# Turned keys of a batch in one row of columns: a change to the two local attention layers of a fused kernel

## The chip, the cores and the metric

The kernel runs as one launch on one core of one Trainium2 chip. The metric is the device time of that launch in microseconds; the kernel before took 1494.41 us (median of three runs, 1487.76 to 1495.81). Names used below: PE is TensorE (PEld its weight loads), DVE is VectorE, ACT is ScalarE, POOL is GpSimd, SP is SyncE, whose queue issues the DMAs. SBUF is the on-chip memory, PSUM the one that matmuls write.

## The reference, cut to what matters

The program is a latent attention with residual, then two "window" layers (local attention and a gated MLP), then a last residual. The change touches only the local attention of the window layers. There are 4 batches of 1024 tokens, width 128, 8 heads of 64, windows of 64 tokens:

```python
def local_attention(q, k, v):                 # WINDOW = 64
    bq = q.reshape(b, h, w, WINDOW, d) * QK_SCALE
    bk = k.reshape(b, h, w, WINDOW, d)
    bv = v.reshape(b, h, w, WINDOW, d)
    def look_around(t):                       # each window sees the one to its left and itself
        p = jnp.pad(t, ((0,0),(0,0),(1,0),(0,0),(0,0)))
        return jnp.concatenate([p[:, :, :w], p[:, :, 1:]], axis=3)
    bk, bv = (look_around(bk), look_around(bv))
    sim = jnp.einsum('bhwid,bhwjd->bhwij', bq, bk)
    mask = (i < j) | (i > j + WINDOW) | (j == -1)
    sim = jnp.where(mask, -jnp.finfo(sim.dtype).max, sim)
    attn = jax.nn.softmax(sim, axis=-1)
    out = jnp.einsum('bhwij,bhwjd->bhwid', attn, bv)
```

Before it q and k are normalised to unit length and rotated (cosine and sine tables); after it come an output projection, a residual, and the MLP.

## The kernel before, in words

`window` (one call per layer, two layers) works on 32 tiles of 128 tokens (two windows each, 8 tiles a batch). Every engine has its own instruction stream, and in each the order is written out by hand in a function `slot(s, ...)`: slot s holds work of several tiles at once (tile s is projected, tile s-2 has its scores, tile s-3 its values, tile s-4 its output). Semaphores alone tie the streams together, and each engine executes its own stream in order.

For a tile the steps are these. PE projects q and k (L892) and v (L896). ACT copies q and k to `raw` (L1006). DVE multiplies `raw` by the cosines (L1133, `cosines`); POOL multiplies it by the sines in four instructions (L1080) and adds the two (L1085, `rotate`). ACT squares and DVE sums (L1124, L1128); POOL raises the sums to the power -1/2 (L1090, `norms`); DVE multiplies the rotated q and k by that (L1142, `normalise`). PE turns q and k so that the 64 numbers of a head lie on partitions (L904, `turn_qk`); ACT copies the turned q (L1022), DVE the turned k (L1148, in `copy_kT`). PE writes the mask (L914) and adds the scores (L921 and L925, `scores`). DVE takes the maxima (L1158), ACT the exponentials (L1029), DVE the reciprocal of the sums (L1168) and the product with it (L1171, both in `divide`). PE turns the probabilities (L936), ACT and DVE copy them (L1036, L1163), and PE multiplies them by v (L951) and by the output weights (L958). DVE adds the result to x (L1175, `residual`).

On DVE a slot runs: `copy_kT(s-2)`, `divide(s-3)`, `residual(s-4)`, `cosines(s)`, first `maxima(s-2)`, `carry(s+2)`, `copy_pT(s-3)`, `normalise(s-1)`, second `maxima(s-2)`, `sums(s)`. On POOL it runs `norms(s-1)` (one L1090), then `rotate(s)` (four L1080, one L1085). `norms` waits for the sums of DVE, `normalise` for `norms`.

The turned keys lie in `kT[P, 2, 4, KEYS]` with KEYS = 192: two buffers that alternate by tile. Columns 0 to 127 are the tile's own two windows; columns 128 to 191 are the second window of the tile before. The second instruction of `copy_kT` (L1151) fetches these 64 columns (of all 4 head pairs, so 256 numbers a partition) out of the other buffer, after a wait for the scores of the tile before, and signals `prev_copied`, for which `scores` waits on PE. The first window of a tile so has its keys in two pieces (own window, then left window) and L921 reads them with a hole in between; the second window's keys are columns 0 to 127. The columns of probabilities, the mask (built on the host) and the values follow that order: `vb` holds for every tile the values of the first window's two pieces, its own on partitions 0 to 63 and the left ones on partitions 64 to 127. Two DMAs a tile (L871, L872, in `spread_v`, on SP's queue) fill it from `v`.

Of the kernel before, what the change touches and what calls it, by code (L numbers as in the profile page):

```python
# [24 lines left out]
B, S, D = 4, 1024, 128  # L25
P = 128
NT = B * S // P
TB = S // P
# [14 lines left out]
DEPTH, HEADS, DH, WIN = 2, 8, 64, 64  # L43
INNER = HEADS * DH
QK_SCALE = 8.0
KEYS = 3 * WIN
# [591 lines left out]
def at_least(eng, sem, base, t, k):  # L638

    if isinstance(t, int) and t + k <= 0:  # L640
        return
    eng.wait_ge(sem, base + t + k)
# [16 lines left out]
def load_mlp_weights(nc, sp, io, sb, layer):  # L659

    w_in, w2, b1 = sb["f_in"], sb["w2"], sb["b1"]
    sp.dma_start(sb["w1"], io["w1"][layer]).then_inc(w_in, 16)
    w2_l = io["w2"][layer]
    sp.dma_start(w2[:, 0:2, :], w2_l[0:2 * HC, :].rearrange("(c p) n -> p c n", p=HC)).then_inc(w_in, 16)
    sp.dma_start(w2[0:HCS[2], 2, :], w2_l[2 * HC:HID, :]).then_inc(w_in, 16)
    b1_l = io["b1"][layer].rearrange("(w n) -> w n", w=2)
    with nc.allow_non_contiguous_dma("a bias to a partition each"):
        for w in range(2):
            for c in range(3):
                sp.dma_start(b1[0:HCS[c], w, c:c + 1], b1_l[w, c * HC:c * HC + HCS[c]].unsqueeze(1)).then_inc(w_in, 16)  # L670
        sp.dma_start(sb["lg"], io["ln_g"][layer].unsqueeze(1)).then_inc(w_in, 16)
        sp.dma_start(sb["lb"], io["ln_b"][layer].unsqueeze(1)).then_inc(w_in, 16)
    sp.dma_start(sb["b2"], io["b2"][bass.ds(layer, 1), :].broadcast_to((P, D))).then_inc(w_in, 16)
    sp.dma_start(sb["shift"], io["c_shift"]).then_inc(w_in, 16)
    sp.dma_start(sb["carry_m"], io["c_carry_m"]).then_inc(w_in, 16)
# [130 lines left out]
def window(nc, io, sb, layer):  # L806
# [5 lines left out]
    base = layer * NT  # L812
    with ExitStack() as ctx:
        def tile(name, shape, dt=F32):
            return ctx.enter_context(nc.sbuf_tensor(f"{name}{layer}", shape, dt))

        def sem(name):
            return sb["kept"]("w_" + name)
# [6 lines left out]
        raw = tile("w_raw", [P, 2, 2 * INNER])  # L825
        t1, t2 = tile("w_t1", [P, 2 * INNER]), tile("w_t2", [P, 2 * INNER])
        rot = tile("w_rot", [P, 2, 2 * INNER])
        qT, kT = tile("w_qT", [P, 2, 4, P]), tile("w_kT", [P, 2, 4, KEYS])
        v = [tile(f"w_v{r}_", [P, INNER]) for r in range(4)]
        vb = [tile(f"w_vb{r}_", [P, INNER]) for r in range(4)]  # L830
        bias = tile("w_bias", [P, 2, HEADS])
# [6 lines left out]
        psT = ctx.enter_context(nc.psum_tensor(f"w_psT_{layer}", [P, 2, 512], F32))  # L838
        psS = ctx.enter_context(nc.psum_tensor(f"w_psS_{layer}", [P, 2, 512], F32))
        psO = ctx.enter_context(nc.psum_tensor(f"w_psO_{layer}", [P, 512], F32))  # L840

        w_in, tables, zeroed = sb["w_in"], sem("tables"), sem("zeroed")
        vb_in = [sem(f"vb_in{r}") for r in range(4)]
        xT_done, hT_copied, carried = sem("xT_done"), sem("hT_copied"), sem("carried")
        qk_done, v_done, sq_done, ss_done, ssm_done, rn_done = (sem(x) for x in ("qk_done", "v_done", "sq_done", "ss_done", "ssm_done", "rn_done"))
        v_copied, raw_done, t1_done, t2_done, rot_done, unit_done = (sem(x) for x in ("v_copied", "raw_done", "t1_done", "t2_done", "rot_done", "unit_done"))
        qkT_done, qT_copied, kT_copied, prev_copied = sem("qkT_done"), sem("qT_copied"), sem("kT_copied"), sem("prev_copied")
        s_done, bias_done, exp_done = sem("s_done"), sem("bias_done"), sem("exp_done")
        rden_done, prob_done = sem("rden_done"), sem("prob_done")
        pT_done, pT_copied = [sem("pT_done0"), sem("pT_done1")], [sem("pT_copied0"), sem("pT_copied1")]  # L850
# [3 lines left out]
        def halves(eng, s, t, k):  # L854

            if isinstance(t, int) and 2 * t + k <= 0:
                return
            eng.wait_ge(s, base * 2 + t * 2 + k)
# [6 lines left out]
        @block.sync  # L865
        def _(sp):
            def spread_v(t, r):

                at_least(sp, v_copied, base, t, 1)
                halves(sp, av_done, t, -4)  # L870
                sp.dma_start(vb[r][0:WIN, :], v[r][0:WIN, :]).then_inc(vb_in[r], 16)  # L871
                sp.dma_start(vb[(r + 1) % 4][WIN:P, :], v[r][WIN:P, :]).then_inc(vb_in[r], 16)  # L872

            sp.wait_ge(zeroed, layer * 4 + 4)
            for t in range(NT):
                if t == 8:
                    load_mlp_weights(nc, sp, io, sb, layer)
                spread_v(t, t % 4)

        @block.tensor  # L880
        def _(pe):
# [25 lines left out]
            def scores(t, r):  # L907
                p = r % 2
                at_least(pe, qT_copied, base, t, 1)
                at_least(pe, kT_copied, base, t, 1)  # L910
                at_least(pe, prev_copied, base, t, 1)
                halves(pe, exp_done, t, 0)
                for w in range(2):
                    pe.matmul(psS[:, w, :].rearrange("p (c k) -> p c k", c=4), sb["ident_b"],  # L914
                              sb["mask_w"][:, t % TB, :].unsqueeze(1).broadcast_to((P, 4, P)), start=True, stop=False, skip_group_check=True)
                for c in range(4):
                    cols = slice(c * P, (c + 1) * P)
                    for w in range(2):
                        rows = slice(DH * w, DH * w + DH)
                        lower = kT[rows, p, c, :].rearrange("p (a k) -> p a k", a=3)[:, 0:3:2, :]  # L920
                        pe.matmul(psS[0:WIN, w, cols].rearrange("p (a k) -> p a k", a=2), qT[rows, p, c, 0:WIN], lower,  # L921
                                  start=False, stop=True, skip_group_check=True)
                    for w in range(2):
                        rows = slice(DH * w, DH * w + DH)
                        i = pe.matmul(psS[WIN:P, w, cols], qT[rows, p, c, WIN:P], kT[rows, p, c, 0:P], start=False, stop=True, skip_group_check=True)  # L925
                i.then_inc(s_done, 2)

            def turn_p(t, r, b):
# [167 lines left out]
        def _(dve):  # L1096

            dve.memset(hT[WIN:P, 1, P:P + 1], 0.0).then_inc(zeroed, 1)
            dve.memset(kT[:, 1, :, :], 0.0).then_inc(zeroed, 1)
            dve.memset(vb[0][WIN:P, :], 0.0).then_inc(zeroed, 1)  # L1100
            dve.memset(ss[:, :, :, 1], 1e-24).then_inc(zeroed, 1)

            dve.wait_ge(w_in, WINDOW_LOADS)
# [38 lines left out]
                dve.tensor_tensor(both, both, rn[:, p, :].unsqueeze(2).broadcast_to((P, 16, DH)), ALU.mult).then_inc(unit_done, 1)  # L1142

            def copy_kT(t, r):
                p = r % 2
                at_least(dve, qkT_done, base, t, 1)
                at_least(dve, prev_copied, base, t, 0)
                dve.tensor_copy(kT[:, p, :, 0:P], psT[:, 1, :].rearrange("p (c n) -> p c n", c=4)).then_inc(kT_copied, 1)  # L1148

                halves(dve, s_done, t, -2)  # L1150
                dve.tensor_copy(kT[:, p, :, P:KEYS], kT[:, 1 - p, :, WIN:P]).then_inc(prev_copied, 1)  # L1151

            def maxima(t, r, w):
                p = r % 2
# [276 lines left out]
def latent_attention_and_window_layers(nc, io):  # L1431
    io["q_parts"] = nc.dram_tensor("q_parts", (B, NG, 3, DK, HG, S), BF16).ap()
    io["k_parts"] = nc.dram_tensor("k_parts", (B, NG, DK, 3, HG, S), BF16).ap()
    with ExitStack() as ctx:
# [53 lines left out]
        for layer in range(DEPTH):  # L1488
            window(nc, io, sb, layer)
            mlp(nc, io, sb, layer)  # L1490
# [3 lines left out]
def constants():  # L1494

    bf, f = mybir.dt.np(BF16), np.float32
    c = {"c_ident": np.eye(P, dtype=f), "c_ident_b": np.eye(P).astype(bf)}
    i, j = np.arange(P)[:, None], np.arange(P)[None, :]
    c["c_mask_q"] = np.where(j > i, NEG, 0.0).astype(bf)
    c["c_mask_k"] = np.where(i > j, NEG, 0.0).astype(bf)  # L1500
    sel = np.zeros((KROWS - ROWS, NG, HG, S), bf)
    for h in range(HG):
        sel[3 * h:3 * h + 3, :, h, :] = 1
    c["c_sel"] = sel


    key = np.where((j >= WIN) & (i < WIN), j - 2 * WIN, j)
    ok = (key <= i) & (i <= key + WIN)
    mask = np.broadcast_to(ok[:, None, :], (P, TB, P)).copy()
    mask[:WIN, 0, WIN:] = False  # L1510
    c["c_mask_w"] = np.where(mask, 0.0, NEG).astype(bf)
    c["c_carry"] = np.broadcast_to((np.arange(TB) > 0).astype(f), (P, TB)).copy()
    c["c_shift"] = np.eye(P, k=1, dtype=f)
    c["c_carry_m"] = np.zeros((P, P), f)
    c["c_carry_m"][P - 1, 0] = 1
    half = np.arange(0, DH, 2, dtype=f)
    inv = (f(1.0) / np.power(f(10000.0), half / f(DH))).astype(f)
    t = np.arange(S, dtype=f)
    freqs = (t[:, None] * inv[None, :]).astype(f)
    base = ((half + f(0.4 * DH)) / f(1.4 * DH)).astype(f)  # L1520
    power = ((t - f(S // 2)) / f(WIN // 2)).astype(f)
    scale = np.power(base[None, :], power[:, None]).astype(f)
    cos, sin = np.cos(freqs).astype(f), np.sin(freqs).astype(f)
    two = lambda a, b: np.concatenate([a, b], axis=-1)
    cosines = np.stack([two(cos * scale, cos * scale) * f(QK_SCALE), two(cos / scale, cos / scale)], 1)
    sines = np.stack([two(-sin * scale, sin * scale) * f(QK_SCALE), two(-sin / scale, sin / scale)], 1)
    for name, x in (("c_cos", cosines), ("c_sin", sines)):
        c[name] = np.ascontiguousarray(x.reshape(TB, P, 2, DH).transpose(1, 0, 2, 3).astype(f))
    return c
# [22 lines left out]
```

## Time and profile before

| | us |
|---|---|
| median of the runs | 1494.41 |
| profiled execution, its own time | 1497.84 |
| its span (first to last instruction) | 1496.1 |
| DVE busy in the span | 1180.9 (79%) |
| POOL busy in the span | 742.3 (50%) |
| PE busy in the span | 1294.6 (87%) |
| ACT busy in the span | 934.8 (62%) |

The shares are averages over the stages. The latent attention runs up to about 590 us; the local attention of the first layer from about 645 to 960 us and of the second from about 1060 to 1378 us, with the MLPs behind them. POOL, 50% busy over the span, is at 9 tenths in the page's slices inside the two local attentions.

### The profile page before, as it was taken

How to read it: one execution, taken by the hardware profiler on the slowest of the kernel's cores; microseconds unless marked ns; L12 is line 12 of the kernel's file. 1: busy time of each engine (PE TensorE's matmuls, PEld its weight loads, DVE VectorE, ACT ScalarE, POOL GpSimd, SP SyncE). 2: the span in 40 equal slices, each digit the busy share in tenths (PEclk: the TensorE clock that was granted, in tenths of full speed). 3: DMA queues.
4: the chain of work that ended last, by engine and by line, in shares of the span. 5: the costliest groups of instructions: out<-in, count | busy, mean ns of one | idle time of the engine just before them, and what ended most of it. 6: DMA issues, size and time to landing. Idle time of an engine off the chain costs nothing. (4 is left out here: it accounts for less than half of the span.)

```text
span 1496.1 us, 30910 instructions
## 1 busy us (share of the span) xinstructions
PE 1294.6 (87%) x11013; PEld 757.0 (51%) x11013; DVE 1180.9 (79%) x2532; ACT 934.8 (62%) x2597; POOL 742.3 (50%) x742
## 2 busy tenths in 40 slices
PE   5479999999999997459999999699689999997892
PEld 3234444444444443326666666565356666665551
DVE  6577888888888860659999999666599999996667
ACT  4416776777677765647888888332378888884230
POOL 2001212211221221469999999310499999993102
PEclk9859999999999997579999999889799999999896
DMA  4412121112111101100211111000002111110001
GB/s 115 132 61 68 35 60 44 37 36 60 43 37 39 33 4 50 50 21 23 51 35 31 30 30 30 8 1 1 21 23 49 30 30 30 34 32 9 1 1 56
DMA packets 35056, 55.40 MB, mean 37 GB/s; under 512 B 7106, under 2 KB 22732, under 8 KB 32588
## 3 DMA queue, kind: packets, MB, share of 16 engines
q1 hardware_dynamic: 34328, 53.27, 13.4%
q8 instruction: 89, 1.46, 0.4%
q14 instruction: 63, 0.52, 0.1%
q10 hardware_dynamic: 576, 0.15, 0.0%
HBM read 26.67 MB, written 8.39 MB: 23 GB/s over the span
## 5 line engine op out<-in xcount | busy, mean ns | idle before, releaser
L595 DVE TENSOR_REDUCE a_nm<-a_psM 128x1 f32<-128x512 f32 (+3 forms) x768 | 372.7, 550 | 101.8 <-PE a_psM L429 54.4
L516 ACT ACTIVATE a_prob<-a_psE 128x512 f32<-128x512 f32 (+3 forms) x768 | 319.4, 499 | 147.9 <-PE a_psE L444 146.1
L429 PE MATMUL a_psM<-a_ks,a_qs 72*128 72x512 bf16 (+3 forms) x768 | 253.0, 343 | 18.7 <-PEq L76 18.1
L444 PE MATMUL a_psE<-a_qs,a_ks 84*128 84x512 bf16 (+3 forms) x768 | 251.9, 336 | 13.2 <-ACT a_prob L516 6.9
L1080 POOL TENSOR_TENSOR w_t<-w_raw,w_sin 128x256 f32<-128x256 f32 x256 | 239.9, 966 | 47.2 <-ACT w_raw L1006 47.2
L551 POOL TENSOR_SCALAR_AFFINE_SELECT a_prob<-a_prob 128x512 f32<-128x512 f32 x128 | 81.1, 635 | 344.4 <-ACT a_prob L516 318.7
L1029 ACT ACTIVATE w_prob<-w_psS,w_bias 128x128 f32<-128x128 f32 x512 | 181.4, 367 | 49.9 <-DVE w_bias L1158 44.4
L1090 POOL TENSOR_TENSOR w_rn<-w_ssm,mhalf 128x16 f32<-128x16 f32 x64 | 189.4, 2960 | 3.1 <-DVE w_ssm L1128 3.1
L1085 POOL TENSOR_TENSOR w_rot<-w_t 128x1024 f32<-128x1024 f32 x64 | 152.0, 2374 | 8.8 <-issue 0.4
L458 PE MATMUL a_psO<-a_prob,v_all 128*32 128x512 f32 (+3 forms) x1536 | 148.1, 502 | 0.0
L444 PEld LDWEIGHTS a_psE<-a_qs,a_ks 84*128 84x128 bf16 x768 | 74.9, 98 | 142.7 <-issue 49.3
L892 PE MATMUL w_psQK<-w_wqkv,w_hT 128*128 128x512 f32 x256 | 130.3, 632 | 4.6 <-DVE w_hT L1119 4.1
L432 PE MATMUL a_psM<-mask_q,ident_b 128*128 128x128 bf16 x512 | 116.3, 228 | 0.0
L1142 DVE TENSOR_TENSOR w_rot<-w_rot,w_rn 128x1024 f32<-128x1024 f32 x64 | 103.1, 1611 | 4.4 <-POOL w_rn L1090 2.7
L1029 ACT ACTIVATION_READ_ACCUMULATOR w_prob<-w_psS,w_bias 128x1 f32 x512 | 104.6, 204 | 0.0
L429 PEld LDWEIGHTS a_psM<-a_ks,a_qs 72*128 72x128 bf16 x768 | 77.7, 101 | 51.8 <-issue 21.4
L1158 DVE TENSOR_REDUCE w_bias<-w_psS 128x4 f32<-128x512 f32 x128 | 87.3, 682 | 6.3 <-PE w_psS L925 6.3
L1133 DVE TENSOR_TENSOR w_t<-w_raw,w_cos 128x1024 f32<-128x1024 f32 x64 | 78.0, 1219 | 16.8 <-ACT w_raw L1006 9.7
L1266 PE MATMUL f_psU<-f_hT,f_w 128*114 128x512 f32 (+1 forms) x192 | 87.9, 608 | 0.0
L1036 ACT ACTIVATE w_pT<-w_psT 128x512 f32<-128x512 f32 x64 | 38.2, 597 | 78.4 <-PE w_psT L936 78.4
L904 PEld LDWEIGHTS w_psT<-ident,w_rot 128*128 128x128 f32 x512 | 60.6, 143 | 48.3 <-issue 29.0
L904 PE MATMUL w_psT<-ident,w_rot 128*128 128x128 f32 x512 | 68.5, 278 | 14.7 <-DVE w_rot L1142 14.6
(139 smaller groups left out, 2508.3 us busy)
## 6 DMA issues: line engine op xcount, KB each, us to landing
w_vb<-w_v SPq DMA_DIRECT2D x128, 128.0 KB, 2.3
a_qs<-q_parts SPq DMA_DIRECT2D x16, 576.0 KB
a_ks<-k_parts SPq DMA_DIRECT2D x16, 576.0 KB
q_parts<-p_parts SPq DMA_DIRECT2D x24, 128.0 KB
k_parts<-p_parts SPq DMA_DIRECT2D x24, 128.0 KB
out_x<-l_y SPq DMA_DIRECT2D x8, 256.0 KB, 2.3
a_qs<-a_nmT SPq DMA_DIRECT2D x32, 48.0 KB
w_wqkv<-in_wqkv SPq DMA_DIRECT2D x2, 768.0 KB, 7.4
```

Source lines behind the costliest of these rows:

```text
L429: mm = pe.matmul(out, qs[0:ROWS, g, j, i * P:(i + 1) * P], ks[0:ROWS, g, j, 512 * kc:512 * kc + n], start=True, stop=not diag)
L432: mm = pe.matmul(out[:, n - P:n], sb["ident_b"], sb["mask_q"], start=False, stop=True)
L444: pe.matmul(psE[:, r % NRING, 0:w], ks[0:KROWS, g, j, kt * P:(kt + 1) * P], qs[0:KROWS, g, j, q0:q0 + w], start=True, stop=True).then_inc( ...
L458: mm = pe.matmul(psO[32 * j:32 * j + 32, q0:512], v_flat[:, col + j * VA:col + j * VA + 32], prob[G % NPROB][:, j, 0:512 - q0], start=(kt ...
L516: act.activation(prob[G % NPROB][:, j, 0:w], psE[:, r % NRING, 0:w], ACT.Exp, scale=SCALE0).then_inc(e_read, 1)
L595: dve.tensor_reduce(nm[:, s % 2, kc, i, j:j + 1], psM[:, r % MRING, 0:n], AX.X, ALU.max, negate=True).then_inc(m_read, 1)
L892: pe.matmul(psQK[:, w, :], hT[:, r % 2, 0:P], wqkv[:, bass.ds(layer * (3 * INNER) + w * INNER, INNER)], start=True, stop=True).then_inc(qk ...
L904: i = pe.transpose(psT[:, w, c * P:(c + 1) * P], rot[:, r % 2, w * INNER + c * P:w * INNER + (c + 1) * P], sb["ident"])
L1029: i = act.activation(prob[:, p, w, c, :], psS[:, w, c * P:(c + 1) * P], ACT.Exp, bias=bias[:, p, n:n + 1], accum_out=den[:, p, n:n + 1])
L1080: i = pool.tensor_tensor(out[:, w, :, half, :], src[:, w, :, 1 - half, :], tab, ALU.mult)
L1085: pool.tensor_tensor(rot[:, r % 2, :], t1[:, :], t2[:, :], ALU.add).then_inc(rot_done, 1)
L1090: pool.tensor_tensor(rn[:, r % 2, :], ssm[:, r % 2, :], sb["mhalf"][:, 0:16], ALU.pow).then_inc(rn_done, 1)
```

## The change

The buffer of the turned keys gets a row of 64 + 1024 columns for a batch, two rows that alternate by batch. `copy_kT` writes each tile's keys once, at its place in that row; the instruction L1151, its wait and the semaphore `prev_copied` are gone. The keys of a window and of the one to its left then lie side by side, and every score matmul reads 128 columns in one piece. The order of columns for the first window becomes left, own; so the mask changes, and `spread_v` puts a tile's first window on partitions 64 to 127 of `vb` and the second on 0 to 63 of the next.

```diff
-        qT, kT = tile("w_qT", [P, 2, 4, P]), tile("w_kT", [P, 2, 4, KEYS])
+        qT, kT = tile("w_qT", [P, 2, 4, P]), tile("w_kT", [P, 2, 4, WIN + S])
...
-                sp.dma_start(vb[r][0:WIN, :], v[r][0:WIN, :]).then_inc(vb_in[r], 16)
-                sp.dma_start(vb[(r + 1) % 4][WIN:P, :], v[r][WIN:P, :]).then_inc(vb_in[r], 16)
+                sp.dma_start(vb[r][WIN:P, :], v[r][0:WIN, :]).then_inc(vb_in[r], 16)
+                sp.dma_start(vb[(r + 1) % 4][0:WIN, :], v[r][WIN:P, :]).then_inc(vb_in[r], 16)
...
-                at_least(pe, prev_copied, base, t, 1)
...
+                half, first = t // TB % 2, t % TB * P
                 for c in range(4):
                     cols = slice(c * P, (c + 1) * P)
-                    for w in range(2):
-                        rows = slice(DH * w, DH * w + DH)
-                        lower = kT[rows, p, c, :].rearrange("p (a k) -> p a k", a=3)[:, 0:3:2, :]
-                        pe.matmul(psS[0:WIN, w, cols].rearrange("p (a k) -> p a k", a=2), qT[rows, p, c, 0:WIN], lower,
-                                  start=False, stop=True, skip_group_check=True)
-                    for w in range(2):
-                        rows = slice(DH * w, DH * w + DH)
-                        i = pe.matmul(psS[WIN:P, w, cols], qT[rows, p, c, WIN:P], kT[rows, p, c, 0:P], start=False, stop=True, skip_group_check=True)
+                    for u in range(2):
+                        for w in range(2):
+                            rows = slice(DH * w, DH * w + DH)
+                            i = pe.matmul(psS[WIN * u:WIN * u + WIN, w, cols], qT[rows, p, c, WIN * u:WIN * u + WIN],
+                                          kT[rows, half, c, first + WIN * u:first + WIN * u + P], start=False, stop=True, skip_group_check=True)
...
-            dve.memset(kT[:, 1, :, :], 0.0).then_inc(zeroed, 1)
-            dve.memset(vb[0][WIN:P, :], 0.0).then_inc(zeroed, 1)
+            dve.memset(kT[:, :, :, 0:WIN], 0.0).then_inc(zeroed, 1)
+            dve.memset(vb[0][0:WIN, :], 0.0).then_inc(zeroed, 1)
...
             def copy_kT(t, r):
-                p = r % 2
                 at_least(dve, qkT_done, base, t, 1)
-                at_least(dve, prev_copied, base, t, 0)
-                dve.tensor_copy(kT[:, p, :, 0:P], psT[:, 1, :].rearrange("p (c n) -> p c n", c=4)).then_inc(kT_copied, 1)
-
-                halves(dve, s_done, t, -2)
-                dve.tensor_copy(kT[:, p, :, P:KEYS], kT[:, 1 - p, :, WIN:P]).then_inc(prev_copied, 1)
+                dve.tensor_copy(kT[:, t // TB % 2, :, WIN + t % TB * P:WIN + t % TB * P + P],
+                                psT[:, 1, :].rearrange("p (c n) -> p c n", c=4)).then_inc(kT_copied, 1)
...
-    key = np.where((j >= WIN) & (i < WIN), j - 2 * WIN, j)
-    ok = (key <= i) & (i <= key + WIN)
+    ok = (i % WIN <= j) & (j <= i % WIN + WIN)
     mask = np.broadcast_to(ok[:, None, :], (P, TB, P)).copy()
-    mask[:WIN, 0, WIN:] = False
+    mask[:WIN, 0, :WIN] = False
```

## Rows read from the trace of the kernel before

**Rows 1.** Windows: us, busy PE, PEld, DVE, ACT, POOL, then PEclk, DMA share, GB/s.
```profile
800.00:880.00 80.00, 77.11 (x845) 50.95 (x843) 78.60 (x114) 65.90 (x215) 78.80 (x53) 1.00 0.14 31
```

**Rows 2.** Groups by line from 600 us: count, busy us, mean ns, idle before.
```profile
L1090 POOL TENSOR_TENSOR w_rn<-w_ssm,mhalf 128x16 f32<-128x16 f32 x64 | 189.4, 2960 | 3.1 <-DVE w_ssm L1128 3.1
...
L921 PE MATMUL w_psS<-w_kT,w_qT 64*64 64x128 f32 x1024 | 72.8, 283 | 0.0
L925 PE MATMUL w_psS<-w_kT,w_qT 64*64 64x128 f32 x1024 | 72.8, 283 | 0.0
...
L1151 DVE COPY w_kT<-w_kT 128x256 f32<-128x256 f32 x64 | 49.9, 780 | 0.0
...
L914 PE MATMUL w_psS<-mask_w,ident_b 128*128 128x512 bf16 x128 | 39.8, 394 | 14.7 <-DVE w_kT L1151 12.6 <-ACT w_qT L1022 2.0
```

**Rows 3.** Timeline, one steady slot: start us, us, engine line op, idle before.
```profile
784.73 2.36 POOL L1085 TENSOR_TENSOR w_rot<-w_t 128x1024 f32<-128x1024 f32 x1
...
785.94 0.69 DVE L1148 COPY w_kT<-w_psT 128x512 f32<-128x512 f32 x1
...
786.55 0.69 DVE L1151 COPY w_kT<-w_kT 128x256 f32<-128x256 f32 x1
...
787.04 2.97 POOL L1090 TENSOR_TENSOR w_rn<-w_ssm,mhalf 128x16 f32<-128x16 f32 x1
787.16 0.19 DVE L1168 RECIPROCAL w_rden<-w_den 128x8 f32<-128x8 f32 x1
787.39 1.22 DVE L1171 TENSOR_TENSOR w_prob<-w_prob,w_rden 128x1024 f32<-128x1024 f32 x1
...
788.53 0.28 DVE L1175 TENSOR_TENSOR xf_sb<-xf_sb,w_psO 128x128 f32<-128x128 f32 x1
...
788.73 1.22 DVE L1133 TENSOR_TENSOR w_t<-w_raw,w_cos 128x1024 f32<-128x1024 f32 x1
...
788.99 0.28 PE L925 MATMUL w_psS<-w_kT,w_qT 64*64 64x128 f32 x2
...
789.86 0.68 DVE L1158 TENSOR_REDUCE w_bias<-w_psS 128x4 f32<-128x512 f32 x1
...
789.98 3.76 POOL L1080 TENSOR_TENSOR w_t<-w_raw,w_sin 128x256 f32<-128x256 f32 x4
...
791.55 1.62 DVE L1142 TENSOR_TENSOR w_rot<-w_rot,w_rn 128x1024 f32<-128x1024 f32 x1
...
793.88 2.37 POOL L1085 TENSOR_TENSOR w_rot<-w_t 128x1024 f32<-128x1024 f32 x1
794.01 1.04 PE L904 MATMUL w_psT<-ident,w_rot 128*128 128x128 f32 x8
...
795.08 0.69 DVE L1148 COPY w_kT<-w_psT 128x512 f32<-128x512 f32 x1
...
796.20 2.96 POOL L1090 TENSOR_TENSOR w_rn<-w_ssm,mhalf 128x16 f32<-128x16 f32 x1
```

**Rows 4.** Timeline of POOL alone, the start-up of the first layer.
```profile
677.64 2.77 POOL L1080 TENSOR_TENSOR w_t<-w_raw,w_sin 128x256 f32<-128x256 f32 x4
680.53 2.36 POOL L1085 TENSOR_TENSOR w_rot<-w_t 128x1024 f32<-128x1024 f32 x1
686.01 2.91 POOL L1090 TENSOR_TENSOR w_rn<-w_ssm,mhalf 128x16 f32<-128x16 f32 x1 [3.11 <-DVE w_ssm L1128]
688.88 4.18 POOL L1080 TENSOR_TENSOR w_t<-w_raw,w_sin 128x256 f32<-128x256 f32 x4
```

**Rows 5.** Timeline of DVE alone, the same stretch.
```profile
680.74 3.24 DVE L1142 TENSOR_TENSOR w_rot<-w_rot,w_rn 128x1024 f32<-128x1024 f32 x1
...
686.44 0.28 DVE L1151 COPY w_kT<-w_kT 128x256 f32<-128x256 f32 x1
```

**Rows 6.** Timeline of DVE alone, near the end of the first layer's attention.
```profile
941.27 1.44 DVE L1151 COPY w_kT<-w_kT 128x256 f32<-128x256 f32 x1
942.63 0.19 DVE L1168 RECIPROCAL w_rden<-w_den 128x8 f32<-128x8 f32 x1
```

**Rows 7.** DMA issues: out, in, queue, operation, count, KB each, median us to landing.
```profile
w_vb<-w_v SPq DMA_DIRECT2D x128, 128.0 KB, 2.3
```

More of the change, by code:

```diff
@@ L846, in window @@
         v_copied, raw_done, t1_done, t2_done, rot_done, unit_done = (sem(x) for x in ("v_copied", "raw_done", "t1_done", "t2_done", "rot_done", "unit_done"))
-        qkT_done, qT_copied, kT_copied, prev_copied = sem("qkT_done"), sem("qT_copied"), sem("kT_copied"), sem("prev_copied")
+        qkT_done, qT_copied, kT_copied = sem("qkT_done"), sem("qT_copied"), sem("kT_copied")
         s_done, bias_done, exp_done = sem("s_done"), sem("bias_done"), sem("exp_done")
```

## The prediction

> **What bounds the kernel now.** I read first the busy time by window inside a local attention, since the shares of the whole span mix stages. In the 80 us from 800 on DVE is busy 78.60, POOL 78.80 and PE 77.11, at full clock [rows 1]. Three engines look full, so the shares can't say which one sets the pace; the timeline of one slot can. The slots repeat: POOL's L1090 starts at 787.04 and again at 796.20, so a slot takes 9.16 us (the window of rows 1 bears it out: 53 instructions of POOL, six a slot, in 80 us). Neither POOL nor DVE waits for a semaphore in such a slot [rows 3]. What they do wait for is each other, inside their instructions:
>
> - L1142 on DVE is issued at 791.55 and takes 1.62 us, where L1133, of the same shape, takes 1.22 [rows 3]. Once it was issued at 680.74, while POOL's L1085 ran from 680.53 to 682.89, and it took 3.24: it ended 1.09 after POOL's instruction had [rows 4, 5]. It waited for that one to finish, and then worked 1.09.
> - The four L1080 take 2.77 us where nothing of DVE's meets them (677.64) and 3.76 where L1142 does [rows 4, 3]: 0.99 lost. So the instruction that POOL has next waits in its turn until L1142 is through. In the slot of rows 3 DVE was asking first (791.55), so it got its turn between the third and the fourth L1080.
> - L1151, the copy that goes, takes 0.28 when POOL is idle or in its L1090 (686.44), and 0.69 in the steady slot: issued at 786.55, with POOL's L1085 running until 787.09, it ends at 787.24 [rows 3 to 5]. Issued earlier still against the same instruction (941.27) it takes 1.44 [rows 6].
> - L1090 is next on POOL. From its start to the first L1080 it takes 2.94 with that copy ahead of it (787.04 to 789.98), and 2.87 without (686.01 to 688.88) [rows 3, 4]: it too waits for what DVE has asked for first, 0.07 here since the copy is short. After that it lets DVE work: L1171, issued 0.35 after its start, takes 1.22, as does L1133 after it [rows 3].
>
> This is one resource with one holder at a time, given in order of asking. The Trainium skill (SBUF — State Buffer, Who interferes with whom) has it as a rule: an instruction of DVE with two SBUF inputs contends with one of GpSimd that reads SBUF, and so does a copy in a fast mode, the later one being fully blocked. The trace agrees, with the 0.99 that POOL loses and the 0.41 and 0.40 that DVE loses above.
>
> So a slot of POOL is 2.94 (L1090) + 3.90 (L1080s to L1085, 789.98 to 793.88) + 2.32 (L1085 to the next L1090) = 9.16, of which 0.99 + 0.07 is spent waiting for DVE. A slot of DVE is 9.14 (L1148 at 785.94 to 795.08), with 0.61 for the copy (786.55 to 787.16, 0.41 of it the wait for POOL) and 0.40 of wait in L1142. Without these each would need 8.1.
>
> **The change, part by part.** *The copy and its order on DVE.* Taking it away gives DVE 0.61 a slot. The naive sum is 64 x 0.61 = 39 us, but POOL paces the slot as much as DVE does, and its next instruction is what matters. Today the copy stands in line behind L1085 in L1171's place: it takes up however early DVE comes, and L1171 is issued only after L1090 has read its input. Without it, DVE goes from L1148 (785.94) by 0.61 and 0.23 (L1168, 787.16 to 787.39) to L1171 at 786.78. POOL's L1085 runs until E = 787.09. L1171 reads two SBUF tiles as L1142 does; it waits until E, ahead of L1090, which POOL issues at E - 0.05, and holds it up for as long as L1142 holds up an L1080: 0.99 in place of 0.07.
>
> Is that a passing meeting or the new rhythm? I carry the rows on, with the distances between DVE's starts of rows 3. L1171 ends at E + 1.08; L1175 starts E + 1.00, L1133 E + 1.20 (L1090 has its turn at 1.08, and lets it work), L1158 E + 2.33, L1142 E + 4.02. POOL: L1090 at E - 0.05, 2.87 + 0.99 later the first L1080 at E + 3.81, to E + 4.53. L1142 waits for that, ends E + 5.61; 1.91 behind its end (793.17 to 795.08) comes L1148, E + 7.52, and L1171 0.84 later, E + 8.36. POOL needs 3.90 from the first L1080: L1085 starts E + 7.71 and ends E + 10.07. L1171 again comes while L1085 runs, 0.65 behind its start and 1.7 ahead of its end. The pattern holds itself, and the slot is 2.87 + 0.99 + 3.90 + 2.32 = 10.08 us: 0.92 more. Where DVE was to gain 0.61, it now stands idle in L1171 for 1.7.
>
> The other engines allow it. The scores of a tile end at 789.27 now (788.99 + 0.28), 0.59 before L1158 takes them up, and PE is through L904 at 795.05, just as L1148 starts [rows 3]; in a slot of 10.08 both have more room. PE's wait for `prev_copied` is hidden in the steady slot, and ends last 12.6 us in all, at the edges of the layers [rows 2].
>
> How many slots: L1171 of tile 0 comes in slot 3, in front of the L1090 of tile 2, so 30 of 32 slots a layer, 60 of the 64 L1090 [rows 2]: 60 x 0.92 = +55.2 us.
>
> *The edges.* At the start of a layer PE waits for the copy (part of the 12.6), which delays the whole chain there; it ends in POOL's wait of 3.11 at 686.01 [rows 4]. Some of that comes back: between 0 and 9 us; I take 4, somewhat more than that one wait.
>
> *Score matmuls.* As many, as large, in the same order of partitions; only the hole in the keys goes. L921, with the hole, and L925, without, take 283 ns each [rows 2]: 0.
>
> *The two DMAs a tile* cross from one half of the partitions to the other. No row shows such a transfer; as they are they land 2.3 us after issue [rows 7], and the values are used three slots after v is copied, some 27 us: hidden, 0, and hidden even at ten times that. SP's queue carries nothing else that is due. *Memsets and mask*: the zeroed part goes from 768 to 512 numbers a partition, once a layer; 0.
>
> Sum: 1497.84 (the profiled execution; 1.7 around its span) + 55.2 - 4 = 1549. That execution stood 3.4 above the median of the runs; on the median's footing it is 1494.4 + 51.2 = 1545.6, and I predict 1545. Its own range, from the edges (0 to -9), 0.88 to 0.96 a slot and the spread of the runs, is 1534 to 1556.
>
> **The rivals.** *L1090 goes ahead of L1171.* For it: no row shows an L1090 behind a long instruction of DVE, only behind the short copy, and its read is 16 numbers. Against it: those 0.07 exist, and are as much less than 0.99 as the copy holds longer or shorter (it ends 0.20 after L1090's start; L1142, at 793.17, ends 1.12 after the start of the fourth L1080, 789.98 + 3 x 0.69). Then POOL's slot is 9.16 - 0.07 = 9.09, DVE stays ahead of it, and the gain is 60 x 0.07 + 4 = 8: 1486. Chance 0.13, half of it inside 0.5% of 1494 (7.5 us, about what a measurement here can tell from none).
>
> *DVE was the pace and the slot shortens.* This is what a count of busy time says: DVE is relieved by 0.61 of 9.16, and POOL's waits for it might fall away too. PE stands next: 77.11 of 80 busy is 8.83 a slot, so at least that is left: (9.16 - 8.83) x 60 = 20, to 1471 with the edges; with all of the 0.61, 1494 - 39 = 1455. Against it: POOL's 8.1 of its own and the 0.99 of L1142, which needs L1090's result and so can't slip under L1090. Chance 0.12 together.
>
> *More of DVE gets in front.* If L1171 came before L1085 starts (it misses by 0.65), it would hold up L1085, and L1133, issued in L1085, would hold up L1090: three holds of 0.99 a slot, 8.1 + 3.0 = 11.1, (11.1 - 9.16) x 60 = +116: 1606 with the edges. It decides at L1142: were it issued before the first L1080 it would be 0.5 earlier, but it waits for the end of L1090, and the L1080 follows that at once. Chance 0.05. The main case keeps 0.70.
>
> **How the numbers follow.** Slower by over 0.5%: 0.70 + 0.05 = 0.75. Within 0.5%: half of the first rival and a little of the edges, 0.08. Faster: 0.17. The range must reach from the main case to the first rival to leave out less than 2 in 10: 1484 to 1558 holds 0.70 x 0.93 + 0.13 = 0.78, and with it part of the second's small end.
>
> **What the profile after would show.** L1171's mean near 2.8 us in place of 1.22, L1090's near 3.9 in place of 2.96, L1090 to L1090 10.08 us; L1080, L1085 and L1133 as now; DVE and PE's busy shares not higher. If L1090 stays near 2.91 and L1171 takes 1.5 or so, the first rival holds; slots under 9 us would say that POOL's waits fell away; an L1085 over 3.3 us is the last one.

## The result, and the profile after

The changed kernel takes 1545.66 us (median of four runs, 1540.98 to 1550.82) where the kernel before takes 1492.26 beside it (four runs): a ratio of 1.0357, 95% interval 1.0329 to 1.0384, so 53 us slower (the interval is 49 to 57). The forecast was 1545, slower, in a range of 1484 to 1558.

The same window of the first local attention, in the columns of [rows 1]:

```profile
800.00:880.00 80.00, 70.25 (x776) 46.69 (x776) 78.70 (x97) 59.08 (x192) 78.94 (x49) 1.00 0.12 28
```

DVE and POOL look as full as before (78.70 and 78.94 against 78.60 and 78.80), at the same clock, but they get less done: 49 instructions of POOL in place of 53, 97 of DVE in place of 114 (of DVE's 13 a slot, one was the copy that went). A busy share that stays while the count falls says that the instructions got longer. The groups by line say which, in the columns of [rows 2] (the line numbers moved: L1090 is L1087 now, L1171 is L1164, L1080 is L1077, L1085 is L1082, L1142 is L1139, L914 is L913, and L921 holds all score matmuls). First three groups of the kernel before that [rows 2] doesn't show, then the changed kernel:

```profile
L1080 POOL TENSOR_TENSOR w_t<-w_raw,w_sin 128x256 f32<-128x256 f32 x256 | 239.9, 966 | 47.2 <-ACT w_raw L1006 47.2
L1085 POOL TENSOR_TENSOR w_rot<-w_t 128x1024 f32<-128x1024 f32 x64 | 152.0, 2374 | 8.8 <-issue 0.4
...
L1171 DVE TENSOR_TENSOR w_prob<-w_prob,w_rden 128x1024 f32<-128x1024 f32 x64 | 78.4, 1225 | 2.2
```
```profile
L1087 POOL TENSOR_TENSOR w_rn<-w_ssm,mhalf 128x16 f32<-128x16 f32 x64 | 245.4, 3834 | 0.0
L1077 POOL TENSOR_TENSOR w_t<-w_raw,w_sin 128x256 f32<-128x256 f32 x256 | 240.9, 971 | 46.2 <-ACT w_raw L1003 46.2
...
L1164 DVE TENSOR_TENSOR w_prob<-w_prob,w_rden 128x1024 f32<-128x1024 f32 x64 | 171.7, 2683 | 2.2
L1082 POOL TENSOR_TENSOR w_rot<-w_t 128x1024 f32<-128x1024 f32 x64 | 151.1, 2360 | 8.8 <-issue 0.4
...
L921 PE MATMUL w_psS<-w_kT,w_qT 64*64 64x128 f32 x2048 | 71.5, 278 | 0.0
...
L913 PE MATMUL w_psS<-mask_w,ident_b 128*128 128x512 bf16 x128 | 39.5, 391 | 5.0 <-ACT w_qT L1019 4.9
```

Two instructions alone are longer: the power instruction on POOL has a mean of 3834 ns against 2960 [rows 2], and DVE's product of the probabilities 2683, where every one of before took 1.22 to 1.23 us. The rest of POOL's work is as it was. In time it looks like this, DVE first, one slot (compare [rows 3]):

```profile
799.32 2.77 DVE L1164 TENSOR_TENSOR w_prob<-w_prob,w_rden 128x1024 f32<-128x1024 f32 x1
...
802.22 1.21 DVE L1130 TENSOR_TENSOR w_t<-w_raw,w_cos 128x1024 f32<-128x1024 f32 x1
...
805.03 1.61 DVE L1139 TENSOR_TENSOR w_rot<-w_rot,w_rn 128x1024 f32<-128x1024 f32 x1
...
808.57 0.69 DVE L1143 COPY w_kT<-w_psT 128x512 f32<-128x512 f32 x1
809.17 0.19 DVE L1161 RECIPROCAL w_rden<-w_den 128x8 f32<-128x8 f32 x1
809.40 2.77 DVE L1164 TENSOR_TENSOR w_prob<-w_prob,w_rden 128x1024 f32<-128x1024 f32 x1
```

and POOL in the same slot:

```profile
798.66 2.36 POOL L1082 TENSOR_TENSOR w_rot<-w_t 128x1024 f32<-128x1024 f32 x1
800.97 3.90 POOL L1087 TENSOR_TENSOR w_rn<-w_ssm,mhalf 128x16 f32<-128x16 f32 x1
804.84 3.76 POOL L1077 TENSOR_TENSOR w_t<-w_raw,w_sin 128x256 f32<-128x256 f32 x4
808.73 2.36 POOL L1082 TENSOR_TENSOR w_rot<-w_t 128x1024 f32<-128x1024 f32 x1
811.05 3.89 POOL L1087 TENSOR_TENSOR w_rn<-w_ssm,mhalf 128x16 f32<-128x16 f32 x1
```

The product is issued at 799.32, in the middle of POOL's addition (798.66 to 801.02), waits for it and ends at 802.09, 1.07 behind it. The power instruction, issued at 800.97, takes 3.90. Slot: 811.05 - 800.97 = 10.08 us. And 64 x (3834 - 2960) ns = 55.9 us is what the power instructions lost; what came back beside it is small.

### The profile page after: what moved, and what is told of

It reads as the page before. It is cut to its first block and busy times, and to the rows that moved or that the text cites. A ratio compares the mean times of both kernels' runs of the same rounds, so it can differ in the third digit from the quotient of the medians.

```text
span 1539.2 us, 30722 instructions
## 1 busy us (share of the span) xinstructions
PE 1291.7 (84%) x11013; PEld 753.5 (49%) x11013; DVE 1229.0 (80%) x2468; ACT 934.8 (61%) x2597; POOL 799.5 (52%) x742
## 5 line engine op out<-in xcount | busy, mean ns | idle before, releaser
L1077 POOL TENSOR_TENSOR w_t<-w_raw,w_sin 128x256 f32<-128x256 f32 x256 | 240.9, 971 | 46.2 <-ACT w_raw L1003 46.2
L1087 POOL TENSOR_TENSOR w_rn<-w_ssm,mhalf 128x16 f32<-128x16 f32 x64 | 245.4, 3834 | 0.0
L1164 DVE TENSOR_TENSOR w_prob<-w_prob,w_rden 128x1024 f32<-128x1024 f32 x64 | 171.7, 2683 | 2.2
L1082 POOL TENSOR_TENSOR w_rot<-w_t 128x1024 f32<-128x1024 f32 x64 | 151.1, 2360 | 8.8 <-issue 0.4
L1139 DVE TENSOR_TENSOR w_rot<-w_rot,w_rn 128x1024 f32<-128x1024 f32 x64 | 103.7, 1621 | 8.8 <-POOL w_rn L1087 7.0
L948 PE MATMUL w_psO<-w_pT,w_vb 128*64 128x64 f32 x1024 | 58.1, 235 | 49.8 <-DVE w_pT L1156 34.3
L933 PE MATMUL w_psT<-ident,w_prob 128*128 128x128 f32 x512 | 71.6, 284 | 25.5 <-DVE w_prob L1164 25.5
L1151 DVE TENSOR_REDUCE w_bias<-w_psS 128x4 f32<-128x512 f32 x128 | 86.8, 678 | 1.1 <-PE w_psS L921 1.1
```

What stands on the lines that cost most here:

```text
L1077: i = pool.tensor_tensor(out[:, w, :, half, :], src[:, w, :, 1 - half, :], tab, ALU.mult)
L1082: pool.tensor_tensor(rot[:, r % 2, :], t1[:, :], t2[:, :], ALU.add).then_inc(rot_done, 1)
L1087: pool.tensor_tensor(rn[:, r % 2, :], ssm[:, r % 2, :], sb["mhalf"][:, 0:16], ALU.pow).then_inc(rn_done, 1)
L1164: dve.tensor_tensor(pr, pr, rden[:, p, :].unsqueeze(2).broadcast_to((P, HEADS, P)), ALU.mult).then_inc(prob_done, 1)
```

## The experiments

All are told against the kernel before, timed on the same chip in the same rounds (its median there 1493.9 to 1494.6).

**e1: the product waits for POOL's addition.** One wait more in the changed kernel, so that the power instruction asks first.

```diff
                 dve.reciprocal(rden[:, p, :], den[:, p, :]).then_inc(rden_done, 1)
+                at_least(dve, rot_done, base, t, min(3, NT - t))
                 at_least(dve, rden_done, base, t, 1)
```

> The changed kernel with one wait more: before its product with the reciprocals, DVE waits until POOL's addition (L1085 before, rotate's last instruction) of the running slot is done. The wait itself should cost DVE nothing that matters, since the product stood behind that addition anyway. Theory (order of asking): the power instruction of POOL is issued before the addition ends and now asks first, so it is no longer held up; a slot of POOL is 2.87 + 3.90 + 2.32 = 9.09 us, the power instruction back at 2.91, the product at about 1.3: 1492 - 60 x 0.07 - 4 = about 1484 to 1488. Rival (the crossing DMAs, the new layout of keys or the mask cost the time): 1546, no change. Rival (the two may not overlap at all, whatever the order): slot about 10, 1540 or more.

Measured: 1487.5 us, ratio 0.9955 (0.9938 to 0.9971). The whole loss is gone by one wait, and some 7 us more: the 0.07 a slot that the copy cost POOL, and the start of the layers. The product on DVE and the power instruction on POOL, two views of one stretch:

```profile
802.88 1.23 DVE L1165 TENSOR_TENSOR w_prob<-w_prob,w_rden 128x1024 f32<-128x1024 f32 x1 [0.46 <-POOL w_rot L1082]
```
```profile
802.81 2.91 POOL L1087 TENSOR_TENSOR w_rn<-w_ssm,mhalf 128x16 f32<-128x16 f32 x1
805.69 3.77 POOL L1077 TENSOR_TENSOR w_t<-w_raw,w_sin 128x256 f32<-128x256 f32 x4
809.59 2.36 POOL L1082 TENSOR_TENSOR w_rot<-w_t 128x1024 f32<-128x1024 f32 x1
811.91 2.91 POOL L1087 TENSOR_TENSOR w_rn<-w_ssm,mhalf 128x16 f32<-128x16 f32 x1
```

The product starts 0.07 behind the power instruction, takes 1.23, and holds nobody up; the slot is 811.91 - 802.81 = 9.10 (9.09 expected). Layout, mask and DMAs are those of the changed kernel, so none of them costs anything that shows here, and the two instructions do overlap if the order is right.

**e2: a copy back in place.** The changed kernel with a copy of L1151's shape in its place, between two places of an unused tile.

```diff
                                 psT[:, 1, :].rearrange("p (c n) -> p c n", c=4)).then_inc(kT_copied, 1)
+                dve.tensor_copy(idle[:, 1, :, P:KEYS], idle[:, 0, :, WIN:P])
```

> The changed kernel with a copy put where L1151 stood, of the same shape (4 x 64 columns of 128 partitions) but between two places of a tile that nothing else uses; nobody waits for it. It is more work than in the changed kernel. Theory (order of asking): it stands behind POOL's addition in place of the product, so the product is issued after the power instruction again: slot 9.16 us, 1492 less the start-up waits of a few us, 1486 to 1492. Rival (crossing DMAs, layout, mask): 1546 or a little above. Rival (DVE's work sets the pace): above 1546.

Measured: 1492.5 us, ratio 0.9992 (0.9975 to 1.0009). Useless work takes the 53 us away. The copy takes 0.71 again and the product behind it 1.23:

```profile
803.38 0.71 DVE L1147 COPY w_idle<-w_idle 128x256 f32<-128x256 f32 x1
...
804.23 1.23 DVE L1167 TENSOR_TENSOR w_prob<-w_prob,w_rden 128x1024 f32<-128x1024 f32 x1
```

**e3: a tiny product in line.** As e2, with a product of 8 columns.

```diff
+                dve.tensor_tensor(idle[:, 0, :], idle[:, 1, :], idle[:, 2, :], ALU.mult)
```

> The changed kernel with a tiny instruction where the copy L1151 stood: a product of two SBUF tiles of 8 columns that nothing uses. Theory (order of asking): what keeps the time down before is not the copy's work but its place in line; the tiny product stands behind POOL's addition as well as the copy did, gives way almost at once, and the power instruction asks before the product with the reciprocals does: slot 9.09 to 9.12 us, 1485 to 1489, a little below the kernel with the full copy (1492.5). Rival (the copy kept DVE back by its length, so 0.2 us of work is needed): the product of the reciprocals is then still ahead, slot 10.08, 1546.

Measured: 1486.5 us, ratio 0.9941 (0.9925 to 0.9958), as fast as e1 within the intervals. The 8 columns take 0.65 us in the steady slot and 0.16 at their shortest; the difference is spent in line behind POOL's addition, which runs until 807.73 + 2.37 = 810.10 (POOL first, then DVE):

```profile
807.73 2.37 POOL L1083 TENSOR_TENSOR w_rot<-w_t 128x1024 f32<-128x1024 f32 x1
```
```profile
809.47 0.65 DVE L1147 TENSOR_TENSOR w_idle<-w_idle 128x8 f32<-128x8 f32 x1
...
810.27 1.22 DVE L1167 TENSOR_TENSOR w_prob<-w_prob,w_rden 128x1024 f32<-128x1024 f32 x1
```

It is the place in line that counts, not the work: the tiny product holds DVE back as long as the copy did because it waits, not because it computes.

**e4 and e6: the product in two and in four pieces.** The changed kernel, the product made by pieces of 4 heads (e4) or 2 heads (e6).

```diff
-                dve.tensor_tensor(pr, pr, rden[:, p, :].unsqueeze(2).broadcast_to((P, HEADS, P)), ALU.mult).then_inc(prob_done, 1)
+                for h in (0, 4):              # e6: (0, 2, 4, 6), two heads each
+                    i = dve.tensor_tensor(pr[:, h:h + 4, :], pr[:, h:h + 4, :], rden[:, p, h:h + 4].unsqueeze(2).broadcast_to((P, 4, P)), ALU.mult)
+                i.then_inc(prob_done, 1)
```

> The changed kernel with the product of DVE made in two instructions of 4 heads (512 columns) each. Theory (order of asking, one holder at a time, for as long as it works): the first half is ahead of the power instruction and holds it up for half as long, 0.55 - 0.13 = 0.42 in place of 0.99; the second half asks after it. Slot 2.87 + 0.42 + 3.90 + 2.32 = 9.51 us: 1492 + 60 x 0.35 - 4 = about 1509. Rival (crossing DMAs, layout): 1546 and a little more, for DVE has 0.1 us a slot more to do. Rival (the power instruction waits for both halves): 1546.

> The changed kernel with the product in four instructions of 2 heads (256 columns). Theory (one holder for as long as it works, in order of asking): the first quarter holds the power instruction up by 0.28 - 0.13 = 0.15 us, where halves held it up by 0.44 and the whole by 0.99; slot 9.09 + 0.15 = 9.24, about 1492 to 1495. Rival (a fixed price for losing the turn, plus a length): between 1500 and 1515. Rival (DVE's added instructions set the pace): above 1515.

Measured: e4 1515.36 us, ratio 1.0142 (1.0113 to 1.0171); e6 1499.37 us, ratio 1.0029 (1.0015 to 1.0043). POOL's power instruction in e4 and then in e6:

```profile
797.64 3.36 POOL L1087 TENSOR_TENSOR w_rn<-w_ssm,mhalf 128x16 f32<-128x16 f32 x1
...
807.19 3.35 POOL L1087 TENSOR_TENSOR w_rn<-w_ssm,mhalf 128x16 f32<-128x16 f32 x1
```
```profile
801.69 3.09 POOL L1087 TENSOR_TENSOR w_rn<-w_ssm,mhalf 128x16 f32<-128x16 f32 x1
...
810.96 3.11 POOL L1087 TENSOR_TENSOR w_rn<-w_ssm,mhalf 128x16 f32<-128x16 f32 x1
```

The hold-up is 3.90 - 2.91 = 0.99 for 1024 columns, 0.45 for 512, 0.19 for 256: 0.54 less for 512 columns and 0.26 less for 256, so about 1 ns a column of the first piece, less a little, with no fixed price. The slots are 9.55 and 9.27 (9.51 and 9.24 expected). The times came out 6 us above e4's expectation and 4 above the top of e6's, and e6's lies 0.6 below the band of its rival, the fixed price. Both expectations had started from 1492 and from slots 0.03 to 0.04 shorter. With the medians beside them, slots averaged over the steady part of a layer (9.15 before, 9.55 in e4, 9.28 in e6) and 3 us back at the start of the layers, the sums are 1494.6 + 60 x 0.40 - 3 = 1515.6 and 1493.9 + 60 x 0.13 - 3 = 1498.7, within 1 us of both. The fixed price falls by the hold-up itself, which shrinks with the piece.

**e5: only the order, in the kernel before.** L1151 moved behind the product; nothing else.

```diff
                 if runs(s - 3):
                     divide(s - 3, r3)
+                if runs(s - 2):
+                    copy_prev(s - 2, r2)      # the second half of copy_kT, moved here
```

> The kernel before with one thing moved: L1151 (the copy of the left window's keys) comes behind the product L1171 on DVE and no longer ahead of it. No layout, DMA, mask or matmul is changed, no work is added or taken. Theory (order of asking): the product now meets POOL's addition first and goes ahead of the power instruction; the slot becomes 10.08 us and the time 1492 + 60 x 0.92 = about 1547; the copy takes its short time. Rival (crossing DMAs, layout, mask): 1492, or some us above as PE gets its keys later.

Measured: 1542.77 us, ratio 1.0329 (1.0304 to 1.0354). The total was met, the place was not. The steady slot, DVE and then POOL:

```profile
803.93 0.69 DVE L1148 COPY w_kT<-w_psT 128x512 f32<-128x512 f32 x1 [0.53 <-PE w_psT L904]
...
804.76 1.23 DVE L1173 TENSOR_TENSOR w_prob<-w_prob,w_rden 128x1024 f32<-128x1024 f32 x1
805.91 0.28 DVE L1153 COPY w_kT<-w_kT 128x256 f32<-128x256 f32 x1
...
806.31 1.22 DVE L1133 TENSOR_TENSOR w_t<-w_raw,w_cos 128x1024 f32<-128x1024 f32 x1
808.14 0.69 DVE L1160 TENSOR_REDUCE w_bias<-w_psS 128x4 f32<-128x512 f32 x1 [0.62 <-PE w_psS L925]
```
```profile
803.62 2.91 POOL L1090 TENSOR_TENSOR w_rn<-w_ssm,mhalf 128x16 f32<-128x16 f32 x1
806.50 3.67 POOL L1080 TENSOR_TENSOR w_t<-w_raw,w_sin 128x256 f32<-128x256 f32 x4
810.30 3.17 POOL L1085 TENSOR_TENSOR w_rot<-w_t 128x1024 f32<-128x1024 f32 x1
```

The power instruction is not held up here (2.91). PE gets its keys later, the scores end later, DVE waits 0.62 and 0.53 for PE and so comes late enough to miss POOL's addition; but now its cosine product (806.31 to 807.53) reaches over the end of the power instruction and holds the first sine product (3.67 for four, against 2.77 free), and the normalisation holds the addition (3.17 against 2.36). Two holds of 0.90 and 0.81 where before there was one of 0.99: a slot of 9.80. POOL waits for no semaphore in it, so these holds are what lengthens it. The meeting that I named came once a layer, at the third power instruction, and was left in the slot behind it:

```profile
674.22 3.90 POOL L1090 TENSOR_TENSOR w_rn<-w_ssm,mhalf 128x16 f32<-128x16 f32 x1
...
686.45 2.91 POOL L1090 TENSOR_TENSOR w_rn<-w_ssm,mhalf 128x16 f32<-128x16 f32 x1 [3.11 <-DVE w_ssm L1128]
```

That slot is 12.23 us: DVE had waited 2.12 for the scores, its normalisation fell 0.44 behind the start of POOL's addition and took 3.00, and POOL then stood still. So the order alone, without any other part of the change, costs about as much, but in the steady slots by two other meetings than the one I named. The expectation met the total by coincidence.

**e7, e8 and e9: can POOL's remaining wait be had?** In e1 POOL still loses 0.99 a slot to the normalisation. e7 multiplies only k by the inverse norm and takes q's into the exponential; e8 leaves q's norm out, to have the same without e7's added instructions; e9 gives one sine product of POOL's to DVE. All three stand on e1.

```diff
 e7, e8
-                dve.tensor_tensor(both, both, rn[:, p, :].unsqueeze(2).broadcast_to((P, 16, DH)), ALU.mult)
+                dve.tensor_tensor(keys, keys, rn[:, p, 8:16].unsqueeze(2).broadcast_to((P, 8, DH)), ALU.mult)
 e7 alone
-                ... bias=bias[:, p, n:n + 1], accum_out=...
+                ... bias=bias[:, p, n:n + 1], scale=rn[:, r, 2 * c + w:2 * c + w + 1], accum_out=...
+                dve.tensor_tensor(bias[:, p, ns], nmax[:, p, ns], rn[:, r, w:8:2], ALU.mult).then_inc(bias_done, 1)
 e9 (POOL's loop over the sine products, then DVE's cosines)
+                        if (half, w) == (1, 1):
+                            continue
 ...
+                dve.tensor_tensor(out[:, 1, :, 1, :], src[:, 1, :, 0, :], tab, ALU.mult).then_inc(t1_done, 1)
```

> The kernel with the wait of e1 and with the normalisation of q moved: DVE multiplies only the keys by the inverse norm (512 columns in place of 1024), the queries' inverse norm goes as a scale into ACT's exponential, and DVE multiplies the 4 maxima by it (two small instructions a slot more). Theory (POOL paces the slot, and what it loses to that instruction is as long as the instruction works): L1142's successor holds POOL up for 0.99 - 0.55 = 0.45; POOL needs 9.09 - 0.54 = 8.55 and PE, at 8.83, becomes the pace: 1487.5 - 0.26 x 60 = about 1472. Rival (DVE or PE paces the slot already, so POOL's loss costs nothing): 1487 or, with the added small instructions in the chain from scores to exponentials, 1490 and more.

> The kernel with the wait of e1, in which DVE's normalisation is left out for q: L1142's successor multiplies the 512 columns of k alone, and q goes on without its norm (that part of the computation is missing here). Nothing else is added, unlike e7, where the small product with two SBUF inputs got stuck behind POOL's addition. Theory (POOL paces the slot; it loses as long as DVE's instruction works): POOL needs 9.10 - 0.54 = 8.56 and PE, at 8.83, becomes the pace: 1487.5 - 0.27 x 60 = about 1471. Rival (PE or DVE paces the slot of e1 already): 1485 to 1488. If it comes out under 1465, PE's floor was set too high.

> The kernel with the wait of e1, and one of POOL's four sine products (256 of 1024 columns) made by DVE right behind its cosine product, that is under the power instruction, where DVE's work with two SBUF inputs holds nobody up. POOL: 9.10 - 0.69 = 8.41 a slot. DVE: 8.13 + 0.28 of its own, about 0.5 of waits for POOL. PE: 8.83. Theory (each engine's own work plus the turns at the port): the pace goes from POOL to PE or DVE, 8.83 to 8.9 a slot, 1487.5 - 0.25 x 60 = about 1472. Rival (DVE's added work moves a hold onto POOL's three products or its addition so that nothing is won): 1485 to 1495.

Measured: e7 1547.16 us (1.0349, 1.0334 to 1.0365), e8 1468.66 us (0.9844, 0.9820 to 0.9868), e9 1584.29 us (1.0610, 1.0581 to 1.0640). e8, which leaves work out, is as the theory has it: the slot is 8.84, with DVE waiting for PE:

```profile
804.16 0.69 DVE L1143 COPY w_kT<-w_psT 128x512 f32<-128x512 f32 x1 [0.92 <-PE w_psT L904]
...
813.00 0.69 DVE L1143 COPY w_kT<-w_psT 128x512 f32<-128x512 f32 x1 [0.92 <-PE w_psT L904]
```

So what POOL waits for DVE in e1 is on the path. In the first slots, where PE's chain is not yet filled, the power instructions stand 8.56 apart, POOL's own sum in the expectation; then PE's 8.83 takes over, DVE comes late by its wait for PE, and POOL loses the difference again in its sine products (3.52 for four). That PE sets the 8.84 is read from DVE's wait for it and from PE's busy time, 77.75 of 80 us; no run took work from PE to show it.

e7 and e9, of which about 1472 was expected as well, show how sharp the edge is. The first three slots of e7 are 8.53 to 8.56 us, as the theory has them, the steady ones 10.22. There its product of 4 maxima, issued at 809.27 behind POOL's addition (808.23), takes 1.60; everything behind it on DVE is late, and POOL then waits for the sums. Both engines:

```profile
809.27 1.60 DVE L1154 TENSOR_TENSOR w_bias<-w_nmax,w_rn 128x4 f32<-128x4 f32 x1
```
```profile
808.23 2.62 POOL L1083 TENSOR_TENSOR w_rot<-w_t 128x1024 f32<-128x1024 f32 x1
812.30 2.91 POOL L1088 TENSOR_TENSOR w_rn<-w_ssm,mhalf 128x16 f32<-128x16 f32 x1 [1.45 <-DVE w_ssm L1126]
```

In e9 POOL is through its three sine products sooner, and the normalisation, issued at 807.52, comes 0.20 too late: the addition started at 807.32. It takes 3.23 us, and POOL stands still for 3.11:

```profile
807.52 3.23 DVE L1144 TENSOR_TENSOR w_rot<-w_rot,w_rn 128x1024 f32<-128x1024 f32 x1
```
```profile
807.32 2.36 POOL L1084 TENSOR_TENSOR w_rot<-w_t 128x1024 f32<-128x1024 f32 x1
812.78 2.91 POOL L1089 TENSOR_TENSOR w_rn<-w_ssm,mhalf 128x16 f32<-128x16 f32 x1 [3.11 <-DVE w_ssm L1127]
```

A slot of 11.02 us: POOL, relieved of 0.69 us of work, lost 1.92 a slot. I had worked out each engine's sum and not carried the slot on, as I had for the prediction; that was the mistake.

## Why the prediction was right

*The mechanism.* The product was to be issued within POOL's addition, wait for its end and hold the power instruction up by 0.99. It did: 2.77 (2.8 forecast), 3.90 (3.9), slot 10.08 (10.08). e1, e2 and e3 take the meeting away in three ways, without touching the rest, and each takes the loss away; e4 and e6 scale it. That is shown, not argued.

*The number.* That 1545.66 lies 0.7 from 1545 is in part luck. The forecast was 1494.4 + 51.2, while the kernel before had a median of 1492.26 beside the changed one: the change costs 53.4, 2.2 more than forecast, and the base was 2.1 lower.

*That it keeps itself up.* L1164 came 0.67 behind the start of the addition (809.40 against 808.73); 0.65 was carried out by hand from [rows 3]. The rhythm set in at the first product in line, with the third power instruction of the layer:

```profile
667.56 2.35 POOL L1082 TENSOR_TENSOR w_rot<-w_t 128x1024 f32<-128x1024 f32 x1
669.86 3.90 POOL L1087 TENSOR_TENSOR w_rn<-w_ssm,mhalf 128x16 f32<-128x16 f32 x1
673.74 3.78 POOL L1077 TENSOR_TENSOR w_t<-w_raw,w_sin 128x256 f32<-128x256 f32 x4
```

*The count.* 60 x 0.92 = 55.2 was forecast, the power instruction's group grew by 55.9. The first two power instructions of a layer stayed at 2.91, the 30 behind them took 3.9.

*The edges.* 4 us back were assumed. PE's wait for the copy, 12.6 in [rows 2], is gone from L913's row, and POOL's wait of 3.11 [rows 4] with it (L1087 has 0.0 idle ahead of it): 55.9 - 3.1 = 52.8, and the medians differ by 53.4. The profiles bear this sum out inside the attentions: from the first to the last power instruction of a layer it was 286.0 and 284.5 us and is 310.6 and 310.8, 50.9 more, and the last one's own 0.93 a layer comes on top. The memsets, put at 0, gave something back too: POOL's wait at the start of a layer was 12.31 and 34.91 us and is 11.83 and 34.40, some 0.5 less each time; e5, with the memsets of before, has 12.31 and 34.90, e2, with a larger one added, 13.07 and 36.01. The two profiled executions differ by less, 1540.98 - 1497.84 = 43.1; 4.8 of that lies ahead of the first attention, where the first sine product starts at 645.47, after 650.29 before, nearly all of it in a part that the change does not touch, and as much again lies between and behind the two attentions, where the executions of e1 to e6 differ among themselves by several us. A comparison of two single executions would have put the sum out by a fifth.

*Score matmuls, DMAs, mask.* The scores take 278 ns each against 283; the DMAs of `v` land after 2.3 us as before [rows 7], though they now cross partitions:

```profile
w_vb<-w_v SPq DMA_DIRECT2D x128, 128.0 KB, 2.3
```

e1 shows that they cost nothing in sum that could be seen.

*The rivals.* "The power instruction goes ahead" fell: its reading of 16 numbers waited as long as a sine product's. "DVE was the pace" fell too: relieved of 0.61 a slot, DVE stood in line for 1.70 (799.32 to 801.02), and its product was 1.55 longer. The case with three holds did not come. e5 qualifies the mechanism: the single hold keeps itself up only where the rest of DVE's slot stays in time; there PE came late, and it lasted one slot.

*The signs.* The durations and the slot came as named. One sign failed: DVE's busy share was to be no higher, and it rose from 79% to 80% of the span (1180.9 us to 1229.0), since an instruction that stands in line counts as busy; PE's fell from 87% to 84%.

## What to carry to other kernels

Two engines that take turns at one resource form a schedule of their own: look not at what an instruction costs but at who asks while whom is working, and carry the new order through a full slot before removing anything; an instruction with 0.28 us of work may be what keeps a long one out of the wrong place. Where an instruction in the trace is longer than the shortest of its form and ends just behind another engine's instruction, that is a wait which no list of waits shows. Having found such a place, fix the order with a wait on a semaphore where the waiting engine has the time (0.46 us a slot on DVE in e1): here the change with one wait more is 0.5% faster than the kernel before, in place of 3.6% slower.

## What the runs showed of the hardware

A product of 8 or of 4 columns on DVE waits for POOL's instruction as a full one does (0.65 us in e3, 1.60 in e7, where the shortest of each takes 0.16). The power instruction on 16 columns lasts 2.91 us, but it met DVE's products only near its start: with a product of 1024 columns in line ahead of it, it took 3.90 (the changed kernel); with the same product issued 0.07 behind it, it took 2.91 and the product its plain 1.23 (e1). The Trainium skill (SBUF — State Buffer, Who interferes with whom) says that order of issue, not shape, decides who blocks; e1 against the changed kernel, the same two instructions in the other order, 2.91 against 3.90, agrees. A bad pattern, once entered, lasts: e9's first three slots took POOL 8.2 to 8.4 us each, until the normalisation fell behind the start of the addition, and then 11.02 each until the last two of the layer. And an exponential on ACT that takes its scale from a tile lasts 0.46 us for 128 columns (e7), where one without took 0.37; that was not counted in e7's expectation either.
